# Causal attention of a four-layer kernel: eight phases of four heads and 512 queries instead of four groups of 1024 queries

## The reference

```
scores = q @ k^T                      # per head, 1024 x 1024, keys up to the query only
probs  = exp((scores - rowmax) / 4)
out    = (probs @ v) / probs.sum()
```

## Time and profile before

| what | us |
|---|---|
| median of three runs | 1034.68 (1032.92 to 1036.53) |
| the profiled execution, its own time | 1038.35 |
| its span in the trace | 1036.6 |
| attention 0, first matmul to end of the last copy | 92.08 to 256.94 |
| attention 1, the same | 398.86 to 563.60 |

### The profile page before, as it was taken

How to read it: one execution, slowest core, us unless ns; L and a number is a source line. 1 busy time by engine, 2 the same in 40 slices (tenths; PEclk the granted TensorE clock), 3 DMA queues, 4 the chain that set the end, 5 groups by cost and what they waited for, 6 DMA issues and landing times. The chain is left out here.

```text
span 1036.6 us, 13091 instructions
## 1 busy us (share of the span) xinstructions
PE 825.3 (80%) x4290; PEld 507.2 (49%) x4290; DVE 662.0 (64%) x1738; ACT 439.3 (42%) x868; POOL 197.3 (19%) x356
## 2 busy tenths in 40 slices
PE   1525798999669976798988699666989999938797
PEld 1422223332558853233323579655556666627686
DVE  5687787780765477788862688745227774256575
ACT  4022267778332151377777453244112222224453
POOL 0533013323010022012322000010601222100053
PEclk9757599999979986599999899876999999969899
DMA  7106400000000056300000700089211111040001
GB/s 236 40 4 230 136 1 1 2 1 1 1 1 1 1 172 213 117 1 1 2 1 1 118 1 1 1 292 376 103 45 31 47 47 41 26 128 1 0 1 41
DMA packets 48568, 63.81 MB, mean 62 GB/s; under 512 B 11542, under 2 KB 33814, under 8 KB 48502
## 3 DMA queue, kind: packets, MB, share of 16 engines
q1 hardware_dynamic: 46630, 57.85, 18.1%
q0 software_dynamic: 1872, 5.13, 1.4%
HBM read 50.30 MB, written 15.51 MB: 63 GB/s over the span
## 5 line engine op out<-in xcount | busy, mean ns | idle before, releaser
L669 ACT ACTIVATE at1probs<-at1scores 128x512 f32<-128x512 f32 (+3 forms) x192 | 83.3, 510 | 28.4 <-PE at1scores L604 27.1
L669 ACT ACTIVATE at0probs<-at0scores 128x512 f32<-128x512 f32 (+3 forms) x192 | 83.3, 510 | 28.0 <-PE at0scores L604 26.7
L960 PE MATMUL f2ps<-gu_raw,f2xT_b 128*128 x184 | 82.9, 593 | 1.0 <-ACT f2xT_b L1035 1.0
L1053 ACT ACTIVATE f2sg<-f2ps 128x512 f32<-128x512 f32 x31 | 18.5, 597 | 137.1 <-PE f2ps L960 100.9
L581 PE MATMUL at1scores<-ks,qs 96*128 96x512 bf16 (+1 forms) x192 | 65.4, 382 | 11.3 <-DMA ks<-scratch 4.9
L581 PE MATMUL at0scores<-ks,qs 96*128 96x512 bf16 (+1 forms) x192 | 65.4, 382 | 11.3 <-DVE at0mx L709 4.6
L709 DVE CUSTOM_DVE_ANT_0 at0scores<-at0scores,at0later 128x128 f32<-128x128 f32 (+3 forms) x128 | 61.2, 505 | 11.7 <-PE at0scores L581 11.5
L709 DVE CUSTOM_DVE_ANT_0 at1scores<-at1scores,at1later 128x128 f32<-128x128 f32 (+3 forms) x128 | 61.2, 504 | 11.7 <-PE at1scores L581 11.5
L604 PE MATMUL at1scores<-qs,ks 99*128 99x512 bf16 (+3 forms) x192 | 57.6, 341 | 10.9 <-ACT at1probs L669 7.4
L604 PE MATMUL at0scores<-qs,ks 99*128 99x512 bf16 (+3 forms) x192 | 57.5, 340 | 10.9 <-ACT at0probs L669 7.4
L697 POOL TENSOR_SCALAR_AFFINE_SELECT at1probs<-at1probs 128x128 f32<-128x128 f32 x128 | 36.3, 292 | 126.6 <-ACT at1probs L669 124.5
(11 more groups left out here) (397 smaller groups left out, 1896.6 us busy)
## 6 DMA issues: line engine op xcount, KB each, us to landing
gu_raw<-in_L_ffn_w_gate_up SPq DMA_DIRECT2D x8, 1024.0 KB, 12.7
scratch<-parts SPq DMA_DIRECT2D x8, 768.0 KB, 4.1
qs<-scratch SPq DMA_DIRECT2D x48, 128.0 KB, 2.7
ks<-scratch SPq DMA_DIRECT2D x48, 128.0 KB, 2.7
dn_raw<-in_L_ffn_w_down SPq DMA_DIRECT2D x8, 512.0 KB, 12.2
f2x_in<-slots_in SPq DMA_DIRECT2D x23, 129.0 KB, 2.1
slots_in<-in_c_empty SPq DMA_DIRECT2D x1, 2944.0 KB, 17.3
traw<-in_L_ffn_w_gate_up SPq DMA_DIRECT2D x1, 2048.0 KB, 11.9
```

The costliest lines, as they stand in the source:

```text
L669: act.activation(probs[:, u % NP, 0:n], unit_bank(u, last)[:, 0:n], ACT.Exp, scale=HD ** -0.5)\
L960: ins = pe.matmul(o, xT_b[:, a % 2, k, :], w, start=(k == 0), stop=(k == KD - 1))
L1053: act.activation(sg[:, u % 2, :], ps[:, u % 2, :], ACT.Silu).then_inc(sgs, 1)
```

## The change

The work is cut into eight phases of four heads (g) by 512 queries (qc).

- Maxima go by phase: 16 units (query tile t, head j), each of one or two chunks, still in three single banks `ps_s`. The mask is now added by PE: a second matmul of 128 columns (`m.above` against the identity) accumulates onto the diagonal block. DVE then uses `tensor_reduce` for every chunk, and POOL makes no mask `later`.
- The parts of a whole phase (four heads, four tiles) are split in five or six DVE operations, turned by one transpose into one of the three `ps_s` banks, copied by ACT to SBUF (`rows`, 48 partitions by 128), and placed into rows 96 to 98 of qs by four DMAs on SP's queue. SP's queue also carries the stacks of groups 1 to 3; the order is now written out.
- Scores of two heads lie in two adjacent banks (`ps_e`, two such pairs), and one ACT instruction takes both exponentials; POOL masks both heads in one instruction. The values have one bank instead of two, so a phase's first values wait for the copy out of the phase before.
- `interleave` now orders maxima over all groups as one list: 25 chunks ahead of the first scores, then two after each unit while the maxima are less than 4200 x 4 columns ahead, and five units at the end of the first phase. The five-bank case of the last group is gone.

```diff
-STEPS = [(qc, kt) for qc in range(NC) for kt in range((qc + 1) * CH // P)]
+PHASES = [(g, qc) for g in range(GROUPS) for qc in range(NC)]
+TILES = CH // P
+PER_PHASE = GH * TILES
+ROW_LAG, EARLY, LEAD = 2, 5, 4200
...
+    while taken < PER_PHASE + EARLY:
+        first.append(i)
+        taken += items[i][0] == "unit" and items[i][2] == 0
+        ahead += chunk_of(*items[i][1:]) if items[i][0] == "unit" else 0
+        i += 1
+    after = []
+    for u in range(GROUPS * NEXP):
+        ahead -= queries_of(u)[1]
+        now = []
+        wanted = EARLY if u == PER_PHASE - 1 else 2 * (ahead < LEAD * GH - CH) if ahead < LEAD * GH else 0
+        while wanted and i < len(items):
...
+            def free(i):
+                if i >= SB:
+                    if ITEMS[i - SB][0] == "unit":
+                        pe.wait_ge(s_red, UNITS_UP_TO[i - SB])
+                    else:
+                        pe.wait_ge(m_out, ROWS_UP_TO[i - SB])
+            def max_unit(i, n, c):
...
+                free(i)
...
+                ins = pe.matmul(ps_s[:, i % SB, 0:width], q, ks[0:STK, g, j, lo:lo + width], start=True, stop=not last)
+                if last:
+                    ins = pe.matmul(ps_s[:, i % SB, width - P:width], m.above[:], m.identb[:], start=False, stop=True)
+                ins.then_inc(s_full, 1)
+            def max_rows(i, p):
+                pe.wait_ge(m_split, p + 1)
+                free(i)
+                turned = ps_s[0:MP * PER_PHASE, i % SB, :].bitcast(BF16)[:, 0:P]
+                pe.transpose(turned, mst[:, p % 2].rearrange("p j i t -> p (j i t)"), m.identb[:]).then_inc(m_turned, 1)
+            def scores(u):
...
+                if j == 0 and kt == 0:
+                    pe.wait_ge(*rows_place(g * NC + qc))
+                if j % 2 == 0 and u // 2 >= TB:
+                    pe.wait_ge(exp_done, u // 2 - TB + 1)
...
+            def values(s):
+                g, (qc, kt) = s // NST, STEPS[s % NST]
+                if kt == 0 and s > 0:
+                    pe.wait_ge(pv_evac, g * NC + qc)
...
+            def rows_out(p):
+                act.wait_ge(m_turned, p + 1)
...
+                act.activation(rows[:, p % 2, :], turned, ACT.Copy).then_inc(m_out, 1)
...
+                act.activation(probs[:, u % NP:u % NP + 2, 0:n], ps_e[:, v % TB, :, 0:n], ACT.Exp, scale=HD ** -0.5)\
+                   .then_inc(exp_done, 1)
+                for p in ROWS_AFTER[u] + ROWS_AFTER[u + 1]:
+                    rows_out(p)
+                if u % NEXP == GH and g > 0:
+                    copy_out(g - 1, 1)
+                if u % NEXP == (TILES + 1) * GH:
+                    copy_out(g, 0)
...
+                pool.affine_select(pair, pair, [[0, 2], [1, P]], ALU.is_ge, 0.0, base=0, channel_multiplier=-1).then_inc(masked, 1)
...
+                dve.tensor_reduce(mx[:, p % 2, k, j, t:t + 1], ps_s[:, i % SB, 0:chunk_of(n, k)], AX.X, ALU.max).then_inc(s_red, 1)
...
+            def place(p):
+                g, qc = PHASES[p]
+                sp.wait_ge(m_out, p + 1)
+                for j in range(GH):
+                    src = rows[j * MP * TILES:(j + 1) * MP * TILES, p % 2, :]
+                    sp.dma_start(qs[STK:STK + MP, g, j, qc * CH:qc * CH + CH], src).then_inc(placed[p % 2], 16)
+            read_group(1)
+            place(0)
+            for n in range(2, 4):
+                sp.wait_ge(m.written[n], 16)
+            read_group(2)
+            place(1)
+            read_group(3)
+            for p in range(2, len(PHASES)):
+                place(p)
```

More of the change, by code:

```diff
@@ new lines, in interleave @@
+def interleave():
+    units = PER_PHASE * len(PHASES)
+    items = []
+    for n in range(units):
+        for c in range((keys_of(n) - 1) // CH + 1):
+            items.append(("unit", n, c))
+        p = (n - ROW_LAG + 1) // PER_PHASE - 1
+        if (n - ROW_LAG + 1) % PER_PHASE == 0 and p >= 0:
+            items.append(("rows", p, 0))
+    items.append(("rows", len(PHASES) - 1, 0))
+    ahead, i, taken = 0, 0, 0
+    first = []
+    while taken < PER_PHASE + EARLY:
[9 more added lines that the diff above has]
+        while wanted and i < len(items):
+            kind, n, c = items[i]
+            now.append(i)
+            i += 1
+            if kind == "unit":
+                ahead += chunk_of(n, c)
+                wanted -= 1
+        after.append(now)
+    while i < len(items):
+        after[-1 - 8].append(i)
+        i += 1
+    return items, first, after
@@ L536, in attention_stage @@
+ITEMS, ITEMS_FIRST, ITEMS_AFTER = interleave()
+UNITS_UP_TO = [sum(item[0] == "unit" for item in ITEMS[:i + 1]) for i in range(len(ITEMS))]
+ROWS_UP_TO = [i + 1 - n for i, n in enumerate(UNITS_UP_TO)]
+ROWS_AFTER = [[ITEMS[i][1] for i in now if ITEMS[i][0] == "rows"] for now in ITEMS_AFTER]
+ROWS_FIRST = [ITEMS[i][1] for i in ITEMS_FIRST if ITEMS[i][0] == "rows"]
 @stage
@@ L574, in _ @@
         @block.tensor
         def _(pe):
[L576 to L604, removed]
-                          start=True, stop=True).then_inc(st_full, 1)
@@ new lines, in values @@
+                    ins = pe.matmul(ps_v[32 * j:32 * j + 32, CH - n:CH], v_all[:, g, kt, j, :], probs[:, u % NP, 0:n],
+                                    start=(kt == 0), stop=(kt == (qc + 1) * TILES - 1))
+                ins.then_inc(pv_done, 1)
+            for i in ITEMS_FIRST:
+                item(i)
+            pe.wait_ge(m.stacked_ones, 16)
+            for u in range(UNITS):
+                scores(u)
+                for i in ITEMS_AFTER[u]:
+                    item(i)
+                if u % GH == GH - 1 and u >= GH:
+                    values(u // GH - 1)
@@ L734, in _, with read_group @@
+            for i, (kind, n, k) in enumerate(ITEMS):
+                if kind == "unit":
+                    maximum(i, n, k)
+                    if n % PER_PHASE == PER_PHASE - 1 and (k + 1) * CH >= keys_of(n):
+                        split_max(n // PER_PHASE)
         @block.sync
         def _(sp):
-            for n in range(2, 4):
-                sp.wait_ge(m.written[n], 16)
-            for g in range(1, GROUPS):
+            def read_group(g):
                 sp.wait_ge(m.stacked, g * STACK_SIGNALS)
```

222 lines of the change are left out of this document (88 added, 134 removed).

## The result

The changed kernel takes 1042.9 us (median of 8 runs, 1037.46 to 1045.79) against 1034.65 of the kernel before in the same session (1032.92 to 1038.91): ratio 1.0066, 95% interval 1.0046 to 1.0087. It is slower by 0.7%, where 980 was forecast. The page of the profiled execution (1045.79 us, the longest of the eight, 2.9 above their median) answers to the earlier trace rows: DVE and ACT have less work, as the change intends, and PE's hardly changed.

What follows compares the result with a forecast made beforehand. The prediction took a PE-ACT handshake to set the period. First score at 104.9, B to 125.4, C 85.5 and D 18.5 end the stage at 229.4 against 256.9; twice 27.5 saved gives 980 (965 to 997; range 955 to 1008).

Steps and rivals of the forecast that it cites:

- step 3: ACT's part: 96 wide exponentials for 192, taken at 0.90 us each in a chain, and 8 copies for 16.
- 4: POOL masks 256 columns in one instruction, between 0.29 and 0.58 us; hidden because values come a step later.
- the paragraph of prices: Costs per column and per instruction for PE, DVE and ACT, derived from rows of the earlier profile.
- part C: Units 16 to 148, to the last maxima: PE's work 75.3 us, with stalls 85.5; DVE 67.
- A: From the stage's start to attention 0's first score: at 104.9 us, where 125.8 stood in the kernel before.
- B: Units 0 to 15 with 35 chunks of maxima, partly at half clock: from 104.9 to 125.4 us.
- D: The last 16,000 columns of exponentials, after the last maxima: 18.5 us, from 15.6 to 19.7.
- Step 7: A phase's transpose waits on PE for DVE's split: about 1 us where the next phase has one-chunk units, 3 us.
- step 6: With one values bank, a phase's first values wait for the copy out: 1.2 us each, 7.2 us over six phases.
- step 5: Rows placed by DMA: about 4.0 us behind a transpose and copy (0.6), on the path only for phases 0 and 1.
- the slower rival: PE's clock stays at 1.2 GHz, each us of PE's work in C and D costing one more: 1166, chance 0.04.
- the handshake stays: Rival: the coupling of PE and ACT persists, C takes 99 us and D 19.7: 1009, chance 0.20.

Runs made afterwards that it cites:

- e8: The kernel before with the mask added by a second matmul on PE and every chunk reduced by plain maximum, nothing else: 1036.78 us, ratio 1.0011.
- e12: The changed kernel with the exponentials of a pair in two instructions, one head at a time: 1046.26 us, ratio 1.0121.
- e5: The changed kernel with six unread matmuls of 512 columns ahead of PE's wait for the split in phases 1, 3, 5 and 7: 1034.29 us.
- e11: e7 with five unread matmuls of 512 columns ahead of PE's wait for the split in phases 1, 3, 5 and 7: 1014.13 us.
- e13: e10 with six unread matmuls of 512 columns ahead of PE's wait for the split in phases 1, 3, 5 and 7: 1010.74 us.
- e10: The changed kernel with one chunk of maxima after each unit as the only edit: 1016.5 us, ratio 0.9836.
- e7: The changed kernel with values copied earlier, rows copied before the wide exponential, rows turned later, split operations spread between reduces: 1015.08 us.
- e9: e7 with one chunk of maxima after each unit from unit 16 on, in place of two or none: 998.35 us, ratio 0.9659.

## Why the prediction was wrong

*The unit prices (step 3, 4 and the paragraph of prices) held.* The reduce of 512 columns has 685 ns for 689; the wide exponential 1.024 us as duration for 1.016 taken; the mask of 256 columns 0.41 us between 0.29 and 0.58; the matmul behind a mask matmul starts 0.06 later (207.30 to 207.36 in the trace). By e8 the mask's move is neutral in the kernel before, and by e12 the wide instruction wins a little, as in step 3. One sum is wrong without effect: for DVE in part C the 84 mask matmuls were counted as its instructions, where 132 chunks are reduced, so 70 us and not 67, still under PE's 75.3.

*A, first score at 104.9: measured 106.6.* The matmuls began at 92.5 as said. The split ended at 100.78 for 100.2 (+0.6). Then the transpose stood on PE behind a maxima unit whose bank came free 1.26 us late, so that the placement began at 102.36, 1.58 us behind the split and not 0.7 (+0.9). The placement itself took 4.25 us for 4.0, though its four issues cost 0.76 each and not 0.47.

*B, 20.5 us: measured 21.6* (106.61 to unit 16's score at 128.16). The clock read 1.00 again behind 112 as forecast; 120 to 128 then ran in part at 0.50, which the forecast did not have.

*D, 18.5 us: measured 25.5.* The windows give 0.87 as mean clock, so (1 − 0.87) / 0.5 x 25.5 = 6.6 us at half clock, which cost at most 3.3; PE also waited 1.21 and 0.80 us for the copy out (239.18, 249.24). Of its wait of 1.85 for the last split, ended at 237.14, 1.7 lie in C.

*C, 85.5 us: measured 109. Here the prediction failed,* and in its sentence that PE's work of 75.3 with the stalls of steps 6 and 7 makes 85.5. It has three parts:

- The stalls. 10.2 us were forecast, and 13.0 are there (4.3 + 3.8 + 3.2, and the 1.7 just named). That the sums are near is luck. Step 7 was right in kind: 3 us forecast, 4.9 there. Of the 7.2 of step 6, the waits for the values' copy, none shows in C. In their place stand 3.8 on the rows' bank, freed behind a wide exponential, which step 5 had left out of the sum, and 4.3 on maxima banks, 3.7 of it in the three waits behind splits.
- The clock. "It rose and then stayed at 1.00 through PE's waits" was the wrong step. The mean of 0.88 over 109 us is 26 us at half clock, which cost up to 13, half of it, if nothing else had held PE up. Single waits of 0.96 in each group had left the kernel before at 1.00; here waits of 1.21 to 1.27 come in pairs 2.8 us apart, three times in C, and half clock follows each pair; of the two single waits of 1.61 it follows one. This is the mechanism of the slower rival, put aside at 0.04 because I asked only whether the clock would stay down throughout; it comes and goes. e5, e11 and e13 show that it costs time by itself; the table below has their price. The Trainium skill ("TensorE: Matmul & The Clock Gate", section "A second HAM failure mode: psum-queue depth-cycling") says that cycling through PSUM banks with frequent short idle times of PE between groups makes its clock swing between the two levels. This trace agrees, with the 0.50 behind waits of 1.26 and 1.27 us; the prediction had weighed the page's other rule only, that on long idle stretches.
- The rest: 109 − 75.3 − 13.0 = 20.7 us are clock and rest together, so at least 7.7 are neither. They are waits too short to appear under modelled ends, or work that costs more than its price. e13 shows about as much with the clock at 1.00 throughout: from unit 16's score at 127.89 to the last transpose at 221.63 are 93.7 us. PE's waits in them are 5.9 and the three sets of filler 18 x 512 / 2400 = 3.8; 93.7 − 75.3 − 5.9 − 3.8 = 8.7. The weight loads show some of it: in part C of e13 they wait 14.9 us for exponentials and 9.8 for maxima. That is the rival "the handshake stays" in part, and "stall-free 75.3" was reached by no version.

What the filler gave, by the traces, both stages together. The times run from the first score to the end of the last copy, and half clock is (1 − clock) / 0.5 of each 2 us from 10 us behind the first score:

| traces | us without, with filler | us of half clock without, with | us won for each us of half clock |
|---|---|---|---|
| changed kernel, e5 | 310.3, 301.2 | 71.7, 40.9 | 0.30 |
| e10, e13 | 282.2, 276.9 | 27.2, 3.4 | 0.22 |
| e7, e11 | 280.4, 275.8 | 17.1, 0 | 0.27 |

So what filler won back is less than the 0.5 that a PE held up by nothing else would win. One reason is in e5's timeline: with the half clock ahead of it gone, PE stands 0.81 us at 126.50 for the placement of the rows, a wait that the slow clock had covered. At these prices, an estimate, the 26 us of part C cost 6 to 8, and not 13.

C's miss of 23.5 is then 2.8 of stalls and 20.7 of clock and short waits together: at most 13 of clock, by the estimate 6 to 8, and the remaining 8 to 15 short waits. Their exact shares in the changed kernel stay open.

*Why the order of one by one is worth 26 us* agrees with all three: it shortens the waits (1.27 on the rows' bank becomes 0.94, 1.25 on a maxima bank 0.85), and by windows of 4 us behind 120 leaves some 14 us of half clock in attention 0 instead of 38. How the gain divides among the three was not measured. The prediction had named "bursts of two chunks after one unit and none after the next" for the handshake rival only, and took the order to be more even than it is.

*The end.* The forecast of 980 is met by no version. The best, e9, needs 146.7 us for the stage (90.2 to 236.9) where 136.9 was forecast (92.5 to 229.4), so 9.8 us more, 19.6 in both, and it is 18 above 980. Its parts in attention 0: 14.3 to the first score (forecast 12.4), 20.3 for B (20.5), 89.0 for C with the end of its wait for the last split left out (124.78 to 213.8; 85.5) and 23.1 for D (18.5), with that wait of 1.82 us at its start. So nearly half of it (4.6) is D, where nothing but exponentials, values and copies is left. Why D takes longer than group 3 did at the same rate per column was not tried.

## What to carry to other kernels

When an order makes the engine that is the bound wait several times in a row, price the clock behind the waits as well as the waits: read the granted clock in short windows (4 us here), not as a mean over the stage, and put unread matmuls into one wait as a test of whether it is clock or wait. Read the effect of such a test from the stage in the trace, and not from the whole time alone. Print the written order before you price it: here the rule "two while behind, else none" made bursts over five units. Spread the producer evenly over the consumer's steps (one chunk after each unit, 26.4 us here), and let the engine that frees a bank do so ahead of its longest instruction (14.2 us). PE's busy time with the known stalls added was a lower bound here, where three engines share few banks: with the clock at 1.00, some 9 us of e13's 93.7 were neither.

## What the runs showed of the hardware that was not expected

- The granted clock fell to 0.50 for 3 to 10 us behind waits of PE of 1.2 to 1.9 us, far shorter than the 3 us gap that the forecast had asked about; yet waits of 0.85 and 0.94 us, 3.6 us apart, left it at 1.00 in e10 (130.98 and 134.56). The length of the wait alone does not decide: e7 has both outcomes behind 0.77 us, and the changed kernel behind 1.61 us, with 0.57 in the 4 us behind 159.33 and 1.00 behind 198.38:

```profile
159.33 0.24 PE L647 MATMUL at0ps_s<-identb,at0mst 128*48 128x128 bf16 x1 [1.61 <-DVE at0mst L755]
...
198.38 0.24 PE L647 MATMUL at0ps_s<-identb,at0mst 128*48 128x128 bf16 x1 [1.61 <-DVE at0mst L755]
```

```profile
160.00:164.00 4.00, 4.00 (x23) 1.56 (x22) 1.85 (x6) 1.16 (x2) 0.41 (x1) 0.57 0.03 7
...
200.00:204.00 4.00, 4.00 (x38) 1.67 (x42) 2.82 (x7) 1.91 (x4) 1.22 (x3) 1.00 0.03 7
```

- 24 more matmuls of 512 columns per stage made the kernel 8.6 us faster by medians, 7.4 by ratios (e5).
- Four small placement DMAs (48 partitions of rows in all) took 3.05 us to issue, 0.76 each, and PE's score came 1.2 us behind the last issue.
